# Constant products in layer 0's cross attention, and a new order of steps and counts, in a four-layer perceiver kernel

## The reference

```python
v = jnp.einsum('bsd,hd->bsh', visual_features, Wv) + bv
t = jnp.einsum('bsd,hd->bsh', text_features, Wt) + bt
dots = jnp.einsum('bih,bjh->bij', v, t)
vn = jnp.linalg.norm(v, axis=-1)
tn = jnp.linalg.norm(t, axis=-1)
denom = jnp.maximum(vn[:, :, None] * tn[:, None, :], EPS)
return dots / denom
```

## Time and profile before

| what | value |
|---|---|
| median of 3 runs | 2608.11 us (2601.25 to 2614.97) |
| the profiled execution | 2616.77 us |
| its span | 2615.5 us |
| mean granted TensorE clock | 0.963 |
| PE busy | 2331.4 us (89%) |
| DVE busy | 1702.6 us (65%) |
| ACT busy | 1340.3 us (51%) |
| POOL busy | 780.3 us (30%) |
| constant products (L471) | 616 |

### The profile page before, as it was taken

The page is one execution under the profiler, slowest core; times in us unless marked ns, Lnnn a source line. Parts: engine busy times, 40 slices in busy tenths (PEclk is TensorE's granted clock), DMA queues, the critical chain, the costliest instruction groups (busy, mean ns, idle before and its releaser), DMA issues.

```text
span 2615.5 us, 62549 instructions
## 1 busy us (share of the span) xinstructions
PE 2331.4 (89%) x26728; PEld 1560.2 (60%) x26728; DVE 1702.6 (65%) x4776; ACT 1340.3 (51%) x2305; POOL 780.3 (30%) x684
## 2 busy tenths in 40 slices
PE   5899999888889998888898888889989888999999
PEld 2566666665545555555576667666645555566666
DVE  4866556667887667768676776666776665655432
ACT  3576445776344338777754444444433566555342
POOL 2322555554121331111012233321210112454434
PEclk8999999999899999999999999999998899999999
DMA  4001442000000000000000000010010000122323
GB/s 124 14 1 37 100 105 60 22 15 11 3 3 6 1 23 37 14 14 2 11 15 19 18 19 19 27 31 14 26 55 8 8 2 2 49 53 53 106 73 89
DMA packets 50454, 84.18 MB, mean 32 GB/s; under 512 B 9536, under 2 KB 24768, under 8 KB 49792
## 3 DMA queue, kind: packets, MB, share of 16 engines
q1 hardware_dynamic: 50176, 80.18, 11.1%
HBM read 77.54 MB, written 2.62 MB: 31 GB/s over the span
## 4 chain that ended last, share of the span: by engine, by line
PE 55%; DVE 22%; ACT 11%; POOL 5%; issue 4%; DMA 2%; SPq 1%; DVEq 0%; POOLq 0%; ACTq 0%
PE psum L938 6%; PE psum L896 5%; PE psum L900 5%; PE psum L1598 3%; PE psum L463 2%; DVE c_L3x_most L1718 2%; PE psum L1691 2%; ACT c_L2x_p L2015 2%; PE psum L471 2%; ACT c_L2x_p L2013 2%; PE psum L1588 1%; PE psum L1387 1%; PE psum L765 1%; PE psum L770 1%; PE psum L1437 1%
## 5 line engine op out<-in xcount | busy, mean ns | idle before, releaser
L471 PE MATMUL psum<-halves_held 128*128 128x512 bf16 x616 | 177.6, 402 | 4.1 <-DVE x_held L635 2.2
L885 POOL TENSOR_TENSOR c_L3f_h<-c_L3f_h,c_L3f_spread 128x512 f32<-128x512 f32 x96 | 120.6, 1283 | 140.6 <-DMA c_L3f_spread<-scratch 107.2
L928 DVE TENSOR_TENSOR c_L3f_h<-c_L3f_h,psum 128x512 f32<-128x512 f32 (+1 forms) x112 | 75.6, 685 | 106.0 <-PE psum L900 77.9
L914 ACT ACTIVATE c_L3f_h<-psum 128x512 f32<-128x512 f32 x112 | 64.7, 594 | 108.2 <-PE psum L896 89.2
L938 PEld LDWEIGHTS psum<-weights,c_L3f_h 128*128 128x128 f32 (+1 forms) x896 | 106.7, 192 | 19.8 <-issue 16.0
L938 PE MATMUL psum<-weights,c_L3f_h 128*128 128x128 f32 (+1 forms) x896 | 109.9, 277 | 1.4 <-POOL c_L3f_h L885 1.4
L471 PEld LDWEIGHTS psum<-halves_held 128*128 128x128 bf16 x616 | 56.1, 101 | 85.1 <-issue 42.1
L896 PE MATMUL psum<-c_L3f_xT,weights 128*128 128x512 f32 x208 | 105.0, 596 | 0.0
L900 PE MATMUL psum<-c_L3f_xT,weights 128*128 128x512 f32 x208 | 104.8, 594 | 0.0
L885 POOL TENSOR_TENSOR c_L0f_h<-c_L0f_h,c_L0f_spread 128x512 f32<-128x512 f32 x64 | 80.5, 1276 | 78.3 <-DVE c_L0f_h L928 50.0
L1598 PE MATMUL psum<-c_L3x_qx,c_L3x_kT 32*128 32x256 f32 x512 | 78.8, 428 | 23.2 <-DVE c_L3x_most L1718 15.7
(11 more groups left out here) (639 smaller groups left out, 6602.2 us busy)
## 6 DMA issues: line engine op xcount, KB each, us to landing
c_L0f_spread<-scratch SPq DMA_DIRECT2D x64, 256.0 KB, 5.3
c_L3f_spread<-scratch SPq DMA_DIRECT2D x32, 512.0 KB, 5.6
c_L2f_spread<-scratch SPq DMA_DIRECT2D x64, 128.0 KB, 3.0
c_L3f_spread<-scratch SPq DMA_DIRECT2D x64, 128.0 KB, 6.1
c_L0x_ctxT<-ctxT SPq DMA_DIRECT2D x8, 384.0 KB, 4.8
c_L1x_ctx<-ctx SPq DMA_DIRECT2D x16, 192.0 KB, 2.4
c_L2x_ctxT<-ctxT SPq DMA_DIRECT2D x8, 384.0 KB, 3.6
c_L3x_ctxT<-ctxT SPq DMA_DIRECT2D x8, 384.0 KB, 3.5
```

Source lines behind the costliest of these rows:

```text
L471: nc.tensor.matmul(j.psum[:, bank, :], j.half["ident"], j.half["take"], start=True, stop=True)
L885: nc.gpsimd.tensor_tensor(h, h, j.m["spread"][:, f, :], ALU.mult).then_inc(*j.up("mixed"))
L928: nc.vector.tensor_tensor(h, h, j.psum[rows, bank, 0:j.tok], ALU.mult).then_inc(*j.up("gated"))
```

## The change

`pe_L0x` gets places for constant products ahead of p1 (bank 1), p2 (bank 1), p3 (bank 0), p4 and p5 (bank 3), and waits for the table of halves, which holds the operands of these products, ahead of p1. `pe_linear` waits in L2a for the job before (`free_bank` waits for `done`, if the job isn't the first of its block) ahead of the products in bank 3. ORDER is written anew, letters and digits. PLAN is unchanged, and so is all other work.

```diff
--- before.py
+++ after.py
@@ -552,27 +552,33 @@
         put = t.matmul(psum[0:64, 2 + h, :], j.weight("wt"), m["ctxT"][:, h * BANK:(h + 1) * BANK], start=True, stop=True)
     put.then_inc(*j.up("keys"))
     yield
+    j.halves(t)
+    pe_warm(nc, j, 1)
     t.wait_ge(*j.at("normed", 1))
     if not j.first:
         t.wait_ge(*j.at("resid", 0))
     pe_turn(nc, j, 0, m["xn"])
     yield
+    pe_warm(nc, j, 1)
     t.wait_ge(*j.at("features", 1))
     t.matmul(psum[0:64, 1, :], j.weight("wv"), m["xT"][:], start=True, stop=True).then_inc(*j.up("queries"))
     yield
     j.cleared(t)
+    pe_warm(nc, j, 0)
     t.wait_ge(*j.at("qx", 1))
     for s in range(j.seqs):
         q = slice(64 * (s % 2), 64 * (s % 2) + 64)
         t.matmul(psum[q, 0, (s // 2) * P:(s // 2 + 1) * P], m["vT"][:, s * S:(s + 1) * S],
                  m["tT"][:, s * SC:(s + 1) * SC], start=True, stop=True)
     yield
+    pe_warm(nc, j, 3)
     t.wait_ge(*j.at("squares", 1))
     for s in range(j.seqs):
         q = slice(64 * (s % 2), 64 * (s % 2) + 64)
         t.matmul(psum[q, 2, (s // 2) * P:(s // 2 + 1) * P], j.c["ones"][:, 0:64], m["t2"][:, s * SC:(s + 1) * SC],
                  start=True, stop=True)
     yield
+    pe_warm(nc, j, 3)
     t.wait_ge(*j.at("squares", 2))
     for n in range(j.tiles):
         put = t.matmul(psum[:, 1, n:n + 1], m["v2"][:, n * P:(n + 1) * P], j.c["ones"][:, 0:1], start=True, stop=True)
@@ -650,6 +656,8 @@
             put = t.matmul(psum[:, bank, n * P:(n + 1) * P], m["xT"][:, n * P:(n + 1) * P], j.weight(w), start=True, stop=True)
         put.then_inc(*j.up("keys"))
     yield
+    if heads == 16:
+        j.free_bank(t)
     pe_warm(nc, j, 3)
     t.wait_ge(*j.at("values", 1))
     t.wait_ge(*j.at("kx", 1))
@@ -2844,76 +2852,76 @@
 ORDER = (
-    "qQddDDpdDlLdkqddDKDpdVPavagpAlGdPapAgppPvvDaAvkvDvpPaPLqdGQpDadPdKlpVVgaApgVppvvdVaVPAPvQkGADvvpPapDgAqdPaddDGPLplDKPaVV"
...
-    "aPApVPvpgApVapvcacvccccccccccccCvsCCCCCCCCCCCCCVS")
+    "qQdddDDpDLldkd9pdDaPaKQqDDvDdglLdVpPa2pAgApGp6PvvavAGvvpP1Pa3Pkg2pqDVa4pVdAaVKpgppdvdvlVadvvVP1PAAGkvpPpAQaPGqdaDPDPDdLd"
...
+    "PgvpVgpaGPvPAgPVpGAPapVPvpgApVapvcavcccccccccccccCvsCCCCCCCCCCCCCVS")
```

More of the change, by code:

```diff
@@ new lines @@
+    "7Pvgv5pVgaDlPKDddpVVVpVpVapaVDpaVGkpVpaPpAvvpPaPkDdLPdLADPAGPAKpvAdlPldDvaPavaPvVVPpAdPvVVApAVAVvvkvPvKvvvVgv9pgPapVVVpa"
+    "VpaVpaVkpVGpVapPpAvDvpPaPAPAdPAddDpADLvlvaGPavaDLPKPDvPVVPpAKPvVVApAVAV7PvvvvvvvVgvPg1pVVVaVpVpadVpVkGpVapaPpAappPvPDAvP"
+    "ADdpPappbrdPrDdrLPrArlADpGPPaKpVpvarpVr+PrrprArvPrrprrBPrrRrrPraAcvPbdRRaspVkDpRsRvPAaPVsRpRRsPvRPRsRDpRRgRRpaRApRgDvARc"
+    "RRVgpgCpBagScavPgSpgcSvVcgSccScGcGPvpAGPaPGVpAGPCLbrprrrprarVPrGrrPDArrrCrrrprrPrrrdcPVbadGsCAKCVsdvClCsGCspCsvpgpagpvpa"
@@ new lines @@
+    "gvVPpAgpaDpvPgpBRRcRDRaRPdvpADRgcRaRRRcRRRPRRpRVRpRRRvPagCcBASPkpScvcgScScPSvVpPGdaAPdGpAPpbrprrrpVarGrCdrPLrrprArVaPrGr"
+    "rPrrCrArvCvrVprGpcCbasPPVspGAPsPVsPGAapVsvCGvCDgpgCaKCgpVgPvpADlcgPPBRRcRRRApRRRPRRRdpRkRRRcDRacRvcRgRRVPpAaCcvBSgpPaSpc"
+    "SvVPgSPAcSVPvGpqAPaGPVdGPAddCVGplPbrGdrpDrrrPraApVprGvPrLprArrPrrdprrCrrDrPrrdVcdClbasCGaACKsPCskVvpGsCCspVgvPQapAgpvgDP"
+    "aDpgpBRvPRgDcRARRaRpLpvRpgRaRRcRRDRcRRpRdRkRPRRdDpVCvcBgaScvcgScPScASKPvPSddpdvPlaqVGppaGApaVpDaGDvdkLCagDCgvKPdPvAPVPvd"
@@ new lines @@
+    "AgCVPPAGPVvPvppGapAPaGVaPApGVCvGCvdDaCCvvCpVQDPPADDVALPa+lPAdvkGPVVAdDDpAGaKpVVvppaaGpqdpapagVV1PdavPdPvAgADA4PlvvddgVDV"
+    "dAdLv8pVvlpaVpa1PaDApVKPvAPVPPADQvDAPDDaPPAvdvkGApALavGkVpDDDapdVDVVvppaapGqdpapaKgVd1PVaPvPAgAvALvPdvDgKVDVAlv8pVdV2Pak"
+    "dvApVpadPapAPVPPAvQAPvdDalPdDPDVALvvADdDGpAavGkVpVa1pVGvppaqdKpdapVadVPPDgAPapAlAdDvLvPaVgVvAvdgVV9PDddAlv1pKVpvPDapAaPa"
+    "VPkpQDAPvPAvDaDPLPAvvAGddpDVAavGkVpVa1pVDGvppaqdapdDKDpVaVPdPlAPApgdAadLvPavVgVvAvgVV9PDAv1pKVpvPdkDapAaPaVPpAQPvPAvDaPd"
@@ new lines @@
+    "VlPAvDvADdGpAavGkVpLVDaVDGKpDdvppaqdapDvddLpVVlPPAPdDApaAgaPvaVgVvAvdgKVV9PAv1pDVpadPkdvlapAPaVPpAQDddPvPAvDaDPLDVPAvvAG"
+    "pAavGkVpVa2pVGvppaqdapDpVaVPDgPAPdDapAdvlAvLPaDDVgVvAvddgKVV9PAv1pKVpvPkaapAPaVPpAdQDPvPAdvDlaDPLPAvDdvADGpADVavGkVpVa1p"
+    "VGKvppadappVaVPDPdLAPApvAdgavPadDKVgVlvAvgVV9PvA1pdVkpvPDapAaPaVPpAPvPAVvaPPAvvADGpAavGVpVVaDGpvvpdaDLpVVpv1PvPAPAvA1Pvg"
+    "gpVVvgADvapVV9PvdAVpKdlPvA1PV+VPDA1PDvPVpVpaVpVGaPGapVApVVvDvLvvGPP3pVVPv1PAPvpApPaApaPapVpDVV2PvvdvkvV1pVvpPaVpPvpAPvAp"
@@ new lines @@
+    "vvAgPvKPpgVgaVVV9PvvVPpAd1PvPVpPv1pVaVpVGaVGVappAPVvDPvvdv1pVdVPlvPAPvpA1pAPaPpVaVPVDaVDdpLkpGvvvDv9pVvpaPKVpdPvpAPvAppv"
+    "vAgPvPgVgaVdVV9PvvdVPpAPvPVpv5pVaVpVGaPlapPVGDpVAv2pvvVvPvvpVpapDDdVPLaGapkp7Pvvvvpvpa1pdAddplvPvAvAPvgPgppVgaV3PvVvvVpV"
+    "DVPv2PAPvpA2pAPaPpVaVVaV6PdKpVpDv5pvvvPvAPvpVpPapVaPVVaGpVkpGvGAvvv9pVPVvPvpVa3pvvvVPaav1PvvvAvvvPvvvvvAvvvvvDApvPvdaPDp"
+    "V2PvVvVVpVpaVddPlPpAaPvgApApaPvPgpVLdVpVaVDPvKgpVp+VvPDgpAkppPvVVvVAv1pAa9pVVVVVVVVVVVVVVVVvVPVVAaPVvPvavdvdPvAvvVvvvPvA"
@@ new lines @@
+    "vvvPvvvvDvDvvVpPaGpPvAVvGpLpaAPapPvVPgdpVGDPGaplKPvPgpVVVpadPvpAgPvgVDpVAVDAkpVVVVpVVVVpVVDVLVVVVVvVVvVvpaPpAvPDvavVavPv"
+    "vvvvvvvPvAVvPAPVvGvvvdPvvdpVPavAGvpAPvvPdVpVGlpaKpaPvPgpGPaPpVpVdvVPgDpAkDPvgVVaVApAVVpVVDVvLpVVgpVVpVVVVVVVvVVVvv1pPAaP"
+    "pDVqvvvPdaavvdvPvAvVvvvvPvAvdvvKPvvVvvGPPAVvGvpPAaPVGPVPGPPVVVPpA2PvQVVpVAvAVVVVpVaVVVVVVVpVaVVVpVVvgpaPvpAVgPlapVDpVPDd"
+    "DvgPALPApVDpvGPgPAKpVpGPvvvPAkdPdVpVGPGaPgPPpVvVpaVpvQqP+avDnAdmDlzPGwPzVwzAPVy8nwgAVxNMZymZnZxymWY4nDWLWx3mGzdXNzwnYMzk"
@@ new lines @@
+    "NzwzmYX3NwyMZZwNwXZnx1MZ2mZyDWWY1MnWxNWyWKnmzz1nxXmz4MwzYwzmXyNwMwwY4NXMxZnWZWMymWNxWWnmZy1nxXmzZz1nZw2MzYwzmzX4NwywwMXn"
+    "xMWWMymWYxNnmynx1mYzWzNwwZZpWNaXpZZZvpMaqpYvpgvXNdaMYdpXNaMYgNmZWWZdPwlnAwPwVPxzQDAmzDzPGxDyPmxAmnwLwVmyDnwGK1PdwwyAnzxz"
+    "2nVzkmzzMxWymNWWx6mZXnwZwZ1myYwnMww1NyXnxMzz1nXmzYMxNzWWzMYNyWmZWZ4NWxX2nZ2MZZyY1mn1NyX1nYMzXNMY1NWWwMwZzZmW3NWWnZX4MZZz"
+    "Y8NzzXwyMw1nwXYMxNWWMWY2NymZWZWNxnXZ9MZZY3NyXnYmMNXMY1NxWWmZZwPwzzApPVPQPAaGP1pAPvqdpAVGpaVgdMDNWpaZpWZWaZX8MvYvmdXlNwnY"
@@ new lines @@
+    "DwMwNXMYDdLxNWWzMgZ1mWkZWzWNxzXm6MDZxZyZmwwmYnwyNwwXnyxnzz2nYmzNxzzYmMxy3mNZwZwnmyXwnMy1nKWWwzz1nw2NxzzzmZyMWxnZWWmyx3mX"
+    "nwwZmyYnMzzwnXNzMYzwzXNwMY4NyWW1MZZxNWnWZmyZWxnym1nxX2mzzwwZpaMYpvpNapYvXdpgMadvXpdNY1Na1MnlWZZWzPgmAz1PzVPywPwwADxP2ndD"
+    "VymDVLnxGAmyPxmAnwwkzmzGNwMnDwKwzx9mzzWyWZxnZWmyZx4mXnwwmyYnMzzwnXwNwMYzXNMY1NxWzWzMZWyZ6NWW1mZXZZMYn3NXMYXNMY1NyWWMZZxn"
+    "WmyNxWW1n4mZXzwZz1nZwYzmMzwNXwwYMX2MxNWWzMY1NWymZZWNWx1nZXZZyMYn4NXyMYmXNMYxWNWnZmZPwzzwApPapVPvAVd+pPadVAVVpAAVvvvadPav"
@@ new lines @@
+    "lavDpVDPDvLdVpkVDvvKv7pVPaApvpPadVPpADvvavPaavVVADpADVLAVDdKPdvlpVvdPvkv1pVVaV2PpAvpPadVPpAdDvvaPavavVVAdDpAlDVAVLdkPvpV"
+    "vPvvVDpVa3pVvpPaApKvavdPavadvVPApdllPvVVApDADADLvvv7pdVVakpPvpVdaPpVvapvVaVpDKPvkpA1PvavgLvpVgv+PdgdAppppPvAvPVVavpdvlPa"
+    "VAAPaVVGplVpvGPVpvGvpvdavPPPPpV4paVpVAvPVgAvDvAgv9pvPaKDpVPrPrVrVbrprVrVPrPrArrPArPrrrDcVpaGbpvspVsaVpvGpaspkVVPvpApaPaP"
+    "RvgPRARPvgPgccBgRVcRcRRRcdARRDRLVRRLRvpPaPCDpBASSapkdvSVKDapPvpGAKGPvaCvgCGPVpvAGVCgvCCgVPADpDppp1PvvAPvaPVAvpPVaaVDVGAp"
@@ new lines @@
+    "VpvGPVpvGvpvdPadvlppapPvdPgPLvvLVglv4pVa2pVApkrPrrVbpArrrrArrrrPrrDrcVpbPssvPVaVasvpVVPpvAPpAgaPKvPgpVpaGpgVcaVvcGDvcgV3"
+    "PcAPcRRRBvpPRaRPRKRd1pRRRRRRaRVCvpBSSApaSkpvPPVAvaPVgPvAPGPAVGCVdpGvGPdvCgACVCgCVPApDdpDpp2PvvAPvaVPvApVPaVaVGAplVPVGvpG"
+    "pvdvlPDvvPPPpVpa1paVpvAVgLkPvvVgALDv5pAapPrrrvbrprVParrPVrVrrPVrprADrprVvcPbPAsasPKpVpsvGpaVpVvGpapVvgPaAvgcPgcRgRcRPBRc"
+    "RRRcRdRRAPRVRRRVvpPaPCPBpKSSAkVPvSApaVdaPPGApVGPvGCAGCVCCCVPpvAagPvAvPvgADDPVAdPdVlpgVVGppVpVGpGPvPDvLPPLvapvPaVapVpvAVP"
@@ new lines @@
+    "vVpAvAvpvDapPapVpPvgPVvVVPvVgAPlPvAvpPaKpVDdpGrrrpVbrprVrGrrdrraVkprrPrarvcvpbApsaspKvppaskPPRVPAPaVPvAPgVPRRvgcBgcRRRPg"
+    "RcAcRRRcRRRRvpCaVPBpSSapSaAVpvpGvGCvGCvPgCAGvadCgvpVgCVPApDDpdppPvvPDavLApVvPadVAAPaVVGpVpvGPVpvGvpvvalPlPLPPpV3paVpvAgv"
+    "PvVgAv3pVavpAprrrPbrrrrprVParrPVrVrdPrVprVAcvPbPAsksPpaVpDvsGpapVpVavGpVvPgAgcaPgcRgRcRPvBRcRRPRRVcRARRDRRVRvpPaPCpBASSa"
+    "pvSVapPvPGApGvCVgvPGPACaVPvGCAvpKgVKCdgCkVPAppppPvvPvaAdpvAPaVPaVApVdVGpvPdpvVvGvpvaVppaGpvlPDgPlPvvPgvvpVa3pVpparVrVArP"
@@ new lines @@
+    "brrrdrDrprArrprvArrcPbksspVPsaPVVvpDVLPVpAgPaPAvgaPgpVpvGcagVcVcvGcLcVPvpVAaPpRRRdBkqRDpRRvaaRRRDRpRRRPRvpAaCvPvBgPSPSAv"
+    "KpVgSVPvPAPgVPAPVdpGAKpGVGCCGCCCVPpdAdDplPvvPvaAVpAADvPaPDVapVVGpvPvVpvGpvvaVLppaGpvPgPvdPvkgPLv3pVaVpprArrVbPrrrVpaAprr"
+    "prvarrvrprrvApcbPsspVaPasPVVDPVpVAgvPvPgAPgpVcaGKcvgVcVcGcVPvgA1PPRRpRVBRvRRRRRRAPaRPRRRCpvBASSVdPSPDVPvpqPaAAPVGpVGvPGC"
+    "AGaCVCvCCVPpAPvAPKVAvPApVpPVaGpVaVPadGVppGv2pvvvPvPPDpvpPapVaVapVApvPvDV1pAAPPVVPVDdvLvPVlVAvP2PAPDvpVGpLaVKpVGaV3PapApP"
@@ new lines @@
+    "vPvVPARvRpVvPvPAPARvpBpRPRadVpRRRRRaRPRRaRDpVPpPvCvBvSv5pSSpapapGvpAGkVGdGCaCgpvvpCaCApVvCaVPvA2PApVdPvAKQqPAvpVpPaVpGVa"
+    "VPadVlppGvDpGvDdvPvvPPPpVVv7pAVPaVpAAaPaPVkppPvDvLvpvVVVDVPvPA1PAKPvpVpGapVVaGV3PapAp1PvvpvRvVPvPAPPAvpRRVpBaRVPRRpRRRaR"
+    "RPRRaPRppCvAvAPvBvS1pVSpSapapPvgGGpAVGdGVCaCpvdCvCpCva1pdVGlQPa+qvAVpVPvPAvpVP4pVAaVpaDPapVpv5pVvvPvv2PAPdDADLpAPPV3PVVv"
```

(13 more changed lines are left out.)

72 lines of the change are left out of this document (4 added, 68 removed).

## The result

The changed kernel takes 2621.73 us, median of 20 runs (2606.52 to 2631.03), against 2606.99 us for before in the same comparison (20 runs, 2594.68 to 2614.97). The ratio is 1.0054, with a 95% interval of 1.0038 to 1.0070: slower by about half a per cent. My forecast was 2597 us, and the time lies just above my range of 2572 to 2620 us. I come back to that gap. Ratios are of fast executions alone, and two slow ones are left out: 7447 us (one of e4) and 7609 us (one of before, in the same call).

What follows compares the result with a forecast made beforehand. TensorE (PE) was taken to bound the kernel, losing time to waits and half clock. L0x's -6.0 and -5 us elsewhere made -11 us, 0.42%: 2597 us from a 2608.11 us median; own range 2585 to 2610, outer 2572 to 2620.

Steps and rivals of the forecast that it cites:

- I take a fifth of the upper end, -5 us: Outside L0x, 184 moved PE steps could give or take 24 us in waits; a gain of 5 us was taken.
- "slower" rival: L1a loses 13 products and L2x 12, so new clock dips could open there: about 2623 us, chance 0.13.
- the first rival: Moved steps elsewhere give most of their 24 us, or L3x's 16 added products close half its dips: 2583 us, chance 0.25.
- The L0x term: 46 products in layer 0's cross attention end the half clock: -8.4 us gained, +2.4 us paid at the head, net -6.0 us.
- The low stretch of the earlier trace: Half clock on PE in L0x from 43.7 to 64.2 us, which the added products were to remove.
- The early start of L0a: L0a's first transposes, at 103.3 us before, were to come near 97 us.
- The lead: The traces were to keep their distance through 430 us; the rest of the gain was to come between 430 and 2260 us.
- The other 37 cost nothing: The L0x products not at the head need 8.9 us of PE, but fall mostly in gaps: cost nothing.
- the two waits cost nothing: Waits for the table of halves in L0x and for done in L2a: cost nothing, the latter at most 4 us.
- The head: Nine products ahead of the first transposes cost 3.7 us; a faster second pair gives 1.3 us back, net +2.4 us.

Runs made afterwards that it cites:

- e4: Order and counts of before up to the last job of L2f, the changed kernel's from there, no products in L0x: 2621.06 us, 1.0035 of before.
- e2: Changed kernel with its order and counts, but without the 46 products in L0x: 2619.29 us, 1.0036 of before.
- e14: Changed kernel without the products in L0x, the kernel of e2 measured again in a later call: 2621.67 us, 1.0037 of before.
- the square: Four kernels on one chip: L0x products or none, new or old order and counts in L3x and L3a; ratios 1.0008, 1.0037, 0.9970, 1.0006.
- e5: Changed kernel without the products in L0x, and with order and counts of before from the last job of L2f on: 2611.60 us, 1.0008 of before.
- e9: Changed kernel's code, with both waits, but order and counts of before and no product in L0x: 2610.12 us, 0.9988 of before.
- e1: Changed kernel's code with order and counts of before, only the 46 products in L0x added: 2621.97 us, 1.0040 of before.
- e17: The kernel of e1 measured again in a later call: order and counts of before plus the 46 L0x products: 2617.11 us, 1.0038 of before.
- e12: Changed kernel without the nine products at the very head, and with the old order and counts from the last job of L2f: 2605.52 us, 0.9971.
- e13: The changed kernel itself, measured again in a later call: 2612.60 us, 1.0008 of before.
- e10: Changed kernel with order and counts of before in the last stage only, from the end of L3a on: 2617.08 us, 1.0010 of before.

## Why the prediction was wrong, point by point

**The step that failed is "I take a fifth of the upper end, -5 us"** for the order and counts outside L0x. Its sign was open in my own text, and it came out the other way. The changed kernel without its products in L0x, which has all of the new order and the other counts, measured 1.0036 (e2) and 1.0037 (e14) of before: +9.4 and +9.7 us where my sum had -5. L3x and L3a make nearly all of it, 8.1 and 9.9 us in the square; e5, with new order and counts up to L3x and no product in L0x, has 1.0008. What the runs show in place of a small gain is the half-clock dip near 1860 us, which comes with the new letters and not with the old ones. The rest of the loss, behind that dip, isn't traced to a cause. The bounds of that term, -24 to +24 us, did hold it; my range did not, because it reached only 12 us above before.

My "slower" rival named 2623 us, close to what was measured, but by luck: its reason was the products that L1a and L2x lose, and the stretch that holds them (25th to 81st) takes 880.2 us in the new order without products in L0x, against 881.1 in the old. L3x's 16 added products I had counted as a hope of the first rival.

**The L0x term was right in the sum, not in its parts.** I had -6.0 us; the square gives -7.6 and -9.4. The low stretch of the earlier trace rows, which I took for the stage's habit, isn't in every execution. Up to the end of L0x the seven kernels without these products have 10.2 to 27.3 us of half clock; the ten with all 46 in the new order have 0.1 us at most. In e9, whose L0x is in the same order as before's, most of the low stretch is missing:

```profile
43.70:64.20 20.50, 17.06 (x107) 10.03 (x106) 15.44 (x39) 9.08 (x18) 11.12 (x8) 0.83 0.22 61
```

Layer 0 takes 427.8 us in before's profile, but 420.4 in e9's and 422.2 in e4's. The products shorten it by 423.9 - 419.4 = 4.5 us in the new order, with 18.7 us less half clock. The rest of their gain, 3 to 5 us, is not made in L0x at all: the 25th to 81st even takes 2.1 us more, and the 81st to 115th, 1000 us later, 5.8 us less (last section). I could not have read that from the stage.

I had also priced the products as if their order were nothing. In the old order (e1, e17) they don't shorten layer 0 at all, 423.9 against 423.5 us, and the new order alone doesn't either, 423.9; only both together reach 419.4. The early start of L0a, which I gave to the products, is mostly the order's: its first transposes come at 97.8 to 103.3 us in the old order without products, at 99.3 and 99.4 with them, at 91.0 to 98.6 in the new order without, and at 90.2 to 92.4 with.

The lead of the changed kernel's profile at the end of layer 0, 427.8 - 419.2 = 8.6 us, was to grow from there to 2260 us. It is gone at the end (2616.56 against 2616.77 us).

**"The other 37 cost nothing" and "the two waits cost nothing"** held within what can be told: in the same 78.6 us PE is busy 5.3 us more, and the stage still ends sooner; e9 has 0.9988.
**The head** cost its 3.73 us, but e12 shows no gain from its removal, and its layer 0 takes 419.2 us where those with the head take 419.4. My +2.4 us as a net cost isn't borne out; a difference of that size is below what these ratios tell.

**What stays open.** The same changed kernel had 1.0054 (from 1.0038 up) in its first comparison and 1.0008 (to 1.0033) in e13's, intervals apart. The parts that I can price sum to zero, as e13 has it; the other 0.46% isn't explained by any run here. e10, which differs from the changed kernel in L3f's order alone, had 1.0010 and supports the lower figure. And e1 and e17, products without their order, are 0.4% slower than before although layer 0 takes as long; their profiles lose 6.0 and 4.7 us in the second and third stretch of the table. There they have 22.8 us more half clock, worth up to 11.4 us, and 2.4 us more of the stalls of the last section. Why products in L0x bring that half clock so much later is not settled.

## What to carry to other kernels

A change under one per cent in a kernel whose executions differ by 1% among themselves can't be sized from one profile of each: look at how the profiled execution stands to the median, and take a stage's half clock for its habit only if several profiles have it. When a whole schedule is written anew, cut it where both schedules have issued the same steps, and time the splices; here that kept the stages that gained and dropped the 0.3 to 0.4% that L3x and L3a lost. A few inserted instructions also move everything behind them in the instruction stream, so test them in the schedule that will be shipped.
